# Second layer of a graph network: softmax chain moved three blocks behind the sums, four sum banks, and another order of stores

## What is computed

```python
h = jnp.maximum(_layernorm(x, axis=-1), 0.0)
m = jax.nn.relu(feat[src]) + EPS            # feat = h
ex = jnp.exp(logits - seg_max[dst])         # logits = m
denom = jax.ops.segment_sum(ex, dst, num_segments=N)
a = ex / denom[dst]
msg = jax.ops.segment_sum(a * m, dst, num_segments=N)
feats = feat + msg
x = x + (feats @ W + b)
```

## Time and profile before

| what | us |
|---|---|
| median of 3 runs | 2431.22 |
| lowest and highest of them | 2426.68, 2435.64 |
| the profiled execution | 2425.77 |
| its span | 2424.0 |
| POOL busy in the span | 1731.9 (71%) |
| DVE busy in the span | 1891.8 (78%) |
| PE busy in the span | 1792.9 (74%) |

### The profile page before, as it was taken

One profiled execution on the slowest core, in us unless ns is written; L12 is line 12 of the kernel. 1 busy time (PEld: TensorE's weight loads), 2 busy tenths in 40 slices (PEclk: granted clock), 3 DMA queues, 4 the chain that ended last, 5 costly groups with the idle time before them and its releaser, 6 DMA issues.

```text
span 2424.0 us, 54194 instructions
## 1 busy us (share of the span) xinstructions
PE 1792.9 (74%) x11221; PEld 1480.3 (61%) x11222; DVE 1891.8 (78%) x4571; ACT 762.8 (31%) x1322; POOL 1731.9 (71%) x1796
## 2 busy tenths in 40 slices
PE   3778777767676766777666767676776766899999
PEld 2466665656555555656555656565555654688887
DVE  8999998878787787887887878887888888454544
ACT  5001112222323333334444444444455556000000
POOL 4777777777777777777777777777777770477774
PEclk9899898988888888888888888888888887999999
DMA  5133444444434445454444445545554444877774
GB/s 165 42 94 91 110 102 104 123 105 113 126 102 124 122 108 137 111 140 127 123 136 128 132 130 139 139 130 137 137 137 136 138 127 142 314 264 270 264 273 149
DMA packets 172472, 344.69 MB, mean 142 GB/s; under 512 B 72689, under 2 KB 126763, under 8 KB 158078
## 3 DMA queue, kind: packets, MB, share of 16 engines
q1 hardware_dynamic: 33378, 153.14, 21.5%
q0 software_dynamic: 60864, 99.55, 17.4%
q10 hardware_dynamic: 77990, 89.82, 10.9%
HBM read 247.65 MB, written 94.68 MB: 141 GB/s over the span
## 4 chain that ended last, share of the span: by engine, by line
POOL 57%; issue 19%; PE 15%; DVE 2%; DMA 2%; ACT 1%; SPq 0%; POOLq 0%; DVEq 0%; ACTq 0%
POOL rows_buf L598 57%; PE ps L864 11%; PE ps L874 2%; DMA rows_buf<-table,index 1%; ACT features_buf L947 0%; PE ps L887 0%; PE ps L679 0%; PE ps L794 0%; DMA final<-residual 0%; DVE ps L1350 0%; PE ps L848 0%; SPq L535 0%; DVE zone L1387 0%; PE ps L881 0%; DMA table<-features_buf 0%
## 5 line engine op out<-in xcount | busy, mean ns | idle before, releaser
L598 POOL DMA_INDIRECT rows_buf<-table,index x1539 | 1493.7, 971 | 495.3 <-issue 492.6
L794 PE MATMUL ps<-zone,planes 128*128 128x400 f16 x2352 | 614.4, 377 | 538.4 <-DVE zone L1387 436.2
L1005 ACT ACTIVATE features_buf<-ps 128x800 f16<-128x800 f32 x392 | 327.8, 836 | 1216.0 <-PE ps L794 1211.1
L1387 DVE TENSOR_SCALAR zone<-iota_c,planes 128x400 f16<-128x400 int16 x2352 | 664.7, 336 | 57.6 <-issue 47.6
L794 PEld LDWEIGHTS ps<-zone,planes 128*128 128x128 f16 x2352 | 250.1, 106 | 715.3 <-issue 657.4
L679 PEld LDWEIGHTS ps<-wet,zone 128*128 128x128 f32 x3136 | 544.9, 248 | 43.6 <-issue 32.5
L679 PE MATMUL ps<-wet,zone 128*128 128x96 f32 x3136 | 531.9, 328 | 8.1 <-DMA zone<-edge_t 8.1
L666 PE MATMUL ps<-onehot,features_buf 128*96 128x128 f32 x3120 | 425.4, 282 | 0.0
L666 PEld LDWEIGHTS ps<-onehot,features_buf 128*96 128x96 f32 x3120 | 392.2, 173 | 11.1 <-issue 0.7
L1350 DVE TENSOR_TENSOR ps<-ps,rows_buf 128x768 f32<-128x768 f32 x171 | 164.6, 962 | 244.1 <-DMA rows_buf<-table,index 216.8
L1148 DVE TENSOR_TENSOR planes<-ps,planes 128x1536 f16<-128x1536 f32 x196 | 341.5, 1742 | 0.0
(11 more groups left out here) (187 smaller groups left out, 785.5 us busy)
## 6 DMA issues: line engine op xcount, KB each, us to landing
counts<-features_buf ACTq DMA_DIRECT2D x392, 200.0 KB
zone<-edge_t SPq DMA_DIRECT2D x98, 768.0 KB
single<-table SPq DMA_DIRECT2D x3072, 0.4 KB
rows_buf<-counts SPq DMA_DIRECT2D x24, 1600.0 KB
rows_buf<-table,index POOLq DMA_INDIRECT x1539
planes<-counts SPq DMA_DIRECT2D x12, 1600.0 KB
table<-planes SPq DMA_DIRECT2D x5, 840.0 KB
final<-residual ACTq DMA_DIRECT2D x48, 48.0 KB
```

The costliest lines, as they stand in the source:

```text
L598: nc.gpsimd.indirect_dma_start(out=into[:, t, :], out_offset=None, in_=table, in_offset=bass.IndirectOffsetOnAxis(ap=at[:, t:t + 1], axis= ...
L794: nc.tensor.matmul(count_ps[:, bass.ds(banks[k], WC)], row_hot[:, u % 2, g * GS + k, :], pair_hot[:, g * GS + k, :], start=False, stop=Fal ...
L1005: nc.scalar.activation(count_out[:, k], bank, ACT.Copy, accum_out=row_sum[:, bass.ds(p, 1)]).then_inc(moved, 1)
L1387: last = nc.vector.tensor_scalar(pair_hot[:, k, :], iota_c[:, :], step_pair[:, bass.ds(i * (IS * SC) + (u * SC + k), 1)], None, ALU.is_equal)
```

## The change

- PE makes `turn` three positions behind the sums instead of one, and `finish` four instead of two (`LAG = 3`). The sums go round four banks (0, 1, 6, 7) and wait for the softmax four positions back; the first four do not wait for any.
- DVE does `softmax(s)` and then `add_aggregate(s-3)` and `add_final(s-4)`. The softmax's result goes to a buffer of four slots, `update`.
- `own` moves from `zone` to `onehot_x`, which is free then, and `own` and `final` have eight slots (`BU`) instead of six.
- SP stores the table pieces first, then all own rows, then the residual. Its two loads of `own` are gone; ACT loads `own` for every position, and six positions ahead.

```diff
-BU = 6
-FEAT = 5760
+BU = 8
+LAG = 3
...
-        own = zone[:, FEAT:FEAT + BU * D].rearrange("p (u d) -> p u d", u=BU)
+        own = onehot_x[:, :, :].rearrange("p a b -> p (a b)")[:, 0:BU * D].rearrange("p (u d) -> p u d", u=BU)
+        block_bank = [0, 1, 6, 7]
...
                 sp.wait_ge(node_out, NG)
                 block_load(1)
+                for u in range(NU - 2):
+                    weighted_store(u)
+                block_load(2)
+                for u in range(NU - 2, NU):
+                    weighted_store(u)
+                for u in range(NU):
+                    own_store(u)
                 for part in (slice(0, EVEN), slice(EVEN, NP)):
                     sp.dma_start(residual.rearrange("(p j) d -> p j d", j=NJ)[part], xs[part, :, :]
                                  ).then_inc(residual_out, 16)
-                for u in range(NU - 2):
-                    own_store(u)
-                weighted_store(0)
-                weighted_store(1)
-                own_store(NU - 2)
-                weighted_store(2)
-                own_store(NU - 1)
-                block_load(2)
-                weighted_store(3)
-                sp.wait_ge(own_out, 2 * NU * 16)
-                sp.wait_ge(step_done, SC + NSTEP)
-                for b in range(2):
-                    sp.dma_start(own[:, b, :], own_rows[b * P:(b + 1) * P, :]).then_inc(residual_in[b], 16)
-                weighted_store(4)
                 for b in range(3, DB):
                     sp.wait_ge(block_ps, 2 + ORDER.index(b - 3) + 1)
                     block_load(b)
...
                     pe.wait_ge(block_in[b % 3], (b // 3 + 1) * 16)
-                    pe.wait_ge(soft_done, s + 1)
+                    if s > LAG:
+                        pe.wait_ge(soft_done, s - LAG + 2)
...
-                turn(0, 0)
-
                 for s in range(2, NB):
                     if ORDER[s] < DB:
                         block_sums(s, ORDER[s])
                     else:
                         fetched_sums(s, ORDER[s] - DB)
-                    turn(s - 1, s - 1)
-                    finish(s - 2, s - 2)
-                turn(NB - 1, NB - 1)
-                finish(NB - 2, NB - 2)
+                    if s >= LAG:
+                        turn(s - LAG, s - LAG)
+                    if s > LAG:
+                        finish(s - LAG - 1, s - LAG - 1)
+                for s in range(NB, NB + LAG):
+                    turn(s - LAG, s - LAG)
+                    finish(s - LAG - 1, s - LAG - 1)
                 finish(NB - 1, NB - 1)
...
-                    if s >= 2:
-                        act.dma_start(own[0:n, s % BU, :], own_rows[rows_at, :]).then_inc(residual_in[s % BU], 16)
+                    act.dma_start(own[0:n, s % BU, :], own_rows[rows_at, :]).then_inc(residual_in[s % BU], 16)
                     act.dma_start(final[0:n, s % BU, :], residual[rows_at, :]).then_inc(residual_in[s % BU], 16)
...
-                softmax(0, 0, 0)
-                softmax(1, 1, 0)
-                add_aggregate(0, 0)
-                for s in range(2, NB):
+                for s in range(NB):
...
                     softmax(s, s, 0)
-                    add_aggregate(s - 1, (s - 1) % 2)
-                    add_final(s - 2, s - 2, 0, min(P, N - ORDER[s - 2] * P))
-                add_aggregate(NB - 1, (NB - 1) % 2)
-                add_final(NB - 2, NB - 2, 0, min(P, N - ORDER[NB - 2] * P))
+                    if s >= LAG:
+                        add_aggregate(s - LAG, (s - LAG) % 2)
+                    if s > LAG:
+                        add_final(s - LAG - 1, s - LAG - 1, 0, min(P, N - ORDER[s - LAG - 1] * P))
+                for s in range(NB, NB + LAG):
+                    add_aggregate(s - LAG, (s - LAG) % 2)
+                    add_final(s - LAG - 1, s - LAG - 1, 0, min(P, N - ORDER[s - LAG - 1] * P))
                 add_final(NB - 1, NB - 1, 0, min(P, N - ORDER[NB - 1] * P))
```

More of the change, by code:

```diff
@@ L209, in gnn_kernel @@
         ln_eps = sb("ln_eps", [P, 2])
-        soft = sb("soft", [P, 2, 4, 2 * D])
+        soft = sb("soft", [P, 2, 3, 2 * D])
+        update = sb("update", [P, LAG + 1, D])
         rows = rows_buf[:, 0:RS * T * D].rearrange("p (s t d) -> p s t d", s=RS, t=T)
@@ L861, in block_sums @@
                     pe.wait_ge(block_in[b % 3], (b // 3 + 1) * 16)
-                    pe.wait_ge(soft_done, s + 1)
+                    if s > LAG:
+                        pe.wait_ge(soft_done, s - LAG + 2)
                     for j in range(NJ):
                         last = nc.tensor.matmul(
-                            ps[:, s % 2, 0:4 * D], blocks[b % 3][0:NP].rearrange("p (d j) -> p j d", j=NJ)[:, j, :],
+                            ps[:, block_bank[s % 4], 0:4 * D], blocks[b % 3][0:NP].rearrange("p (d j) -> p j d", j=NJ)[:, j, :],
                             table16[0:NP, j, :], start=(j == 0), stop=(j == NJ - 1))
@@ L871, in fetched_sums @@
                     pe.wait_ge(fetch_hot_done, g + 1)
-                    pe.wait_ge(soft_done, s + 1)
+                    if s > LAG:
+                        pe.wait_ge(soft_done, s - LAG + 2)
                     for k in range(FETCH[g]):
-                        last = nc.tensor.matmul(ps[:, s % 2, 0:4 * D], fetch_hot[g % 2][:, k, :],
+                        last = nc.tensor.matmul(ps[:, block_bank[s % 4], 0:4 * D], fetch_hot[g % 2][:, k, :],
                                                 fetched[g % 2][:, k, :], start=(k == 0), stop=(k == FETCH[g] - 1))
@@ L880, in turn @@
                     pe.wait_ge(soft_added, b + 1)
-                    nc.tensor.transpose(ps[0:D, 2 + u % 2, 0:P], soft[:, u % 2, 3, 0:D], ident[:, :]
+                    nc.tensor.transpose(ps[0:D, 2 + u % 2, 0:P], update[:, u % (LAG + 1), :], ident[:, :]
                                         ).then_inc(soft_turned, 1)
@@ L1547, in softmax @@
                     dve.wait_ge(block_ps, b + 3)
-                    found = ps[:, slot, 0:4 * D].rearrange("p (q h d) -> p q h d", q=2, h=2)
+                    found = ps[:, block_bank[u % 4], 0:4 * D].rearrange("p (q h d) -> p q h d", q=2, h=2)
                     nc.vector.tensor_copy(soft[:, slot, 1, :].rearrange("p (q d) -> p q d", q=2),
@@ L1564, in softmax @@
                     dve.wait_ge(soft_step[4], b + 1)
-                    nc.vector.scalar_tensor_tensor(soft[:, slot, 3, 0:D], total, 1.0 / P_SCALE,
+                    nc.vector.scalar_tensor_tensor(update[:, u % (LAG + 1), :], total, 1.0 / P_SCALE,
                                                    soft[:, slot, 2, D:2 * D], ALU.mult, ALU.mult
@@ L1569, in softmax @@
                     dve.wait_ge(residual_in[u % BU], (i + (u // BU + 1)) * 32)
-                    nc.vector.tensor_tensor(soft[:, slot, 3, 0:D], soft[:, slot, 3, 0:D], own[:, u % BU, :], ALU.add
+                    nc.vector.tensor_tensor(update[:, u % (LAG + 1), :], update[:, u % (LAG + 1), :], own[:, u % BU, :], ALU.add
                                             ).then_inc(soft_done, 1)
```

## The result

| | before | changed |
|---|---|---|
| median of 22 runs each, us | 2431.39 | 2437.87 |
| lowest and highest | 2425.28, 2437.36 | 2432.27, 2441.37 |
| span of the profiled execution | 2424.0 | 2434.2 |

The ratio is 1.0024, with a 95% interval of 1.0016 to 1.0032: 5.8 us slower, 3.9 to 7.8 (the two medians lie 6.5 us apart). The forecast was +4.3 us, 2435.5, within half a per cent.

The account below looks back on a forecast made before the run. PE was taken to set the pace in the second layer's steady part, so only the ends could change. The terms 3.3 + 0 + 1.0 gave +4.3 us, from 2431.22 to 2435.5 us, range 2425.6 to 2445.

Parts of the forecast that it names:

- The change does what it says: Rival, start of second layer: block 3 arrives in time, gain capped near 4 us, -3 with the end, 2428; chance 0.12.
- the idle time: Sign, PE before position 3: one idle time of 12 to 16 us, ended by block 3's DMA.
- the lower clock: Sign, position 3 after the stall: its first 3 us run at clock 0.50.
- The last sums near 2419.7: Sign, end of the second layer: the last sums near 2419.7 us, with four copies behind the last softmax.
- Term 1: Start of second layer: late block 3 moves position 4 from 2103.45 to 2106.75, +3.3 us (bounds -1.6 and +11.7).
- Term 2: Steady part of second layer: 0 us, since the four banks remove waits that were not there.
- Term 3: End, behind the last softmax: four copies and five additions instead of two and three, +1.0 us.
- Sharing: Rival, block 3's load: gathers and ACT's loads take turns with SP's queue; 2440.5 us, or 2443.9 at low rate; chance 0.20.
- late loads: Rival, softmax 0: twelve loads instead of eight compete with block 3, softmax done after 2106.7; 2437 us; chance 0.06.
- The cover for `turn(0)`: Start: softmax 0 done at 2100, ahead of the `turn(0)` of 2106.7 by over 6 us.
- lands some 3 us later: 40th gather, if block 3 came in time: issued at 2133.9, landing some 3 us later; PE would ask at 2128.4.
- the gain is capped near 4 us: Gathers limit any faster start: 3 us from the gathers' earlier start, about 1 of slack.

Follow-up runs that it names:

- e4: Changed kernel with the residual store put back into the gap ahead of the table pieces: 2428.02 us, 0.9991 of the kernel before.
- e3: Changed kernel with the load of count block 3 ahead of the own rows and the residual: 2443.35 us, 1.005 of the kernel before.
- e5: Changed kernel with 85 unused matmuls keeping PE busy while it waits for block 3: 2432.13 us, 1.0004 of the kernel before.
- e10: Changed kernel with turns and finishes caught up over the last positions, shortening the end: 3779.46 us on another chip, 0.9981 of the kernel before.
- e1: Changed kernel's lag of three and four banks, with the store order of before: 2434.46 us, 1.0021 of the kernel before.
- e6: e1 with every second gathered block one position later in the order: 2426.38 us, 0.9988 of the kernel before.
- e7: Changed kernel with own rows in the gap, residual last, and each engine waiting only for what it needs: 2426.68 us, 0.9991 of the kernel before.
- e8: e7 with the gathered-block order of e6: 2425.95 us, 0.9989 of the kernel before.
- e2: Changed kernel's store order with the chain of before (one block behind, two banks): 2446.42 us, 1.0068 of the kernel before.
- e9: e4 with the gathered-block order of e6 and a shorter end: 3778.78 us on another chip, 0.9978 of the kernel before.

## Why the prediction was right, and where its sizes were off

**The mechanism held step by step.** Position 2 ran at once at full clock. The stall moved behind it and became longer; SP's list put block 3 behind everything; the gap of the DMA engines stood empty. e4 moves one store into the gap and gets 8.7 us back at position 4, and e3 shows that exchanging block 3 with what stands ahead of it doesn't help. *The change does what it says* (0.12) fell with that. The number alone would not have told this mechanism from others: any cost of the start up to about +11 us stays within half a per cent. The rows tell it. Of the signs listed, the idle time was just longer than forecast (16.2 us, not 12 to 16) and the lower clock lasted nearly 6 us, not 3. "The last sums near 2419.7" fits only their end by the forecast's own +3.3 (2416.54 + 3.3); they ended at 2422.75 aligned.

**Term 1, forecast +3.3, measured +6.2.** Two parts:

- The start of position 3: 2097 forecast, 2098.4 aligned measured. The first table piece was issued at the same aligned time (2058.07 less 2.88 is 2055.19), so block 3 was there 41.5 us behind the first byte. The window of these 41.5 us, columns as in the earlier trace rows:

```profile
2059.80:2101.29 41.49, 25.26 (x146) 20.39 (x145) 12.96 (x29) 9.41 (x17) 10.18 (x11) 0.83 0.96 335
```

335 GB/s are 13.9 MB: the 12.88 of the forecast and 1.0 of others, where 0.8 had been estimated. So the sum as it was worked out, 2098.1 at 332 GB/s, was right within 0.3 us, and the miss is the step behind it, the choice of 2097 because the end might run at 366. By an estimate from the 358 GB/s that the Trainium skill's "DMA: Bandwidth & Descriptors", section "Specifications", gives as a core's limit to HBM, the 12.88 MB would have been there 5.5 us earlier than they came; the 335 GB/s of this window lie below that figure, and the 416 and 401 of two short windows below lie above it. +1.4.
- The cold clock. I took position 3's 9.73 us from the stall of before. It took 11.29. Windows of the changed kernel (PE busy, granted clock, DMA share, GB/s):

```profile
2101.00:2103.00 2.00, 1.71 (x6) 0.50 1.00 416
...
2105.00:2107.00 2.00, 2.00 (x8) 0.50 0.99 401
2107.00:2109.00 2.00, 2.00 (x12) 0.91 1.02 367
```

The 1.2 GHz level (0.50) lasts until about 2107, nearly 6 us, where it was 3 before. The cost above 8.29 is 3.0 us instead of 1.44, and e5 shows that it is the clock: 8.34 us warm. +1.5.

**Term 2, 0, held**: from position 4 to the last sums are 310.49 us in both traces, and the four banks removed nothing. **Term 3, +1.0, measured +1.1**; e10 takes it away.

**Sharing (0.20) did not happen, and late loads (0.06) came near.** The engines' time by queue in the changed kernel (packets, MB, share; q1 is SP's, q0 POOL's, q10 ACT's), first from 2088 to 2101, while block 3 moves, then from 2101 to 2107, when all three queues move packets throughout; the third fence is the kernel before, from 2082 to 2085:

```profile
q1 hardware_dynamic: 323, 4.10, 89.5%
q0 software_dynamic: 160, 0.35, 7.4%
q10 hardware_dynamic: 48, 0.02, 0.5%
```
```profile
q1 hardware_dynamic: 178, 2.05, 81.3%
q0 software_dynamic: 183, 0.38, 16.3%
q10 hardware_dynamic: 182, 0.06, 4.0%
```
```profile
q1 hardware_dynamic: 362, 1.07, 95.4%
q10 hardware_dynamic: 300, 0.10, 13.1%
```

SP's queue kept nine tenths, not a half. From 2101 to 2107 the three queues moved 178, 183 and 182 packets: as many each, but with SP's about 11.5 KB long, the gathers' 2.1 and ACT's 0.4, the shares were 81, 16 and 4%. The Trainium skill's rule that an engine takes turns packet by packet ("DMA: Bandwidth & Descriptors", "Queues, rings and completion order") agrees with these counts. But turns of unequal packets are no equal shares, which was my error in reading it. The loser is ACT, whose queue moves about 30 packets a microsecond there, where before, beside SP's packets of 3 KB, it moved 100. Softmax 0 needs the first two loads, 256 rows of 384 bytes. In DVE's timeline its wait for them ends here:

```profile
2109.89 0.26 DVE L1567 TENSOR_TENSOR update<-update,onehot_x 128x96 f32<-128x96 f32 x1 [32.36 <-DMA final<-residual]
```

That is 13.7 us after the issue of `final` at 2096.21, where it was 8.1 before (2084.59 less the 2076.46 of the earlier trace rows); in e5 it is 14.7. The cover for `turn(0)` at 2112.42 was 2.3 us, not "over 6". e5 uncovers it: with position 3 three microseconds shorter, `turn(0)` waits. The packet counts of the two traces show the starving; no run changed a packet size by itself.

**A wrong step that did not come to bear:** a gather's landing. I wrote that the 40th "lands some 3 us later". In e1 it took 6.9, with the same order of gathers. In the changed kernel PE reaches those sums only at 2149.83, so it didn't matter; but "the gain is capped near 4 us" was still too kind: e1, with a start 2.2 us ahead of before and gathers 1.5 us behind it (2089.07, aligned 2089.40, against 2087.89), ended 4.7 us slower. With gathers this near, a faster start of PE is given back.

Why e1's gather took 6.9 us where that of before took at most 3.9, no run tested, but the traces point to the same turns. In e1 SP issues a count block at 2138.13, together with that gather, and from 2138.8 to 2144.5 its 1.64 MB hold 80.2% of the engines' time while the gathers move 126 packets. Before, the block next to it had been issued at 2132.19, 4.6 us ahead of the gather, and from 2136.8 to 2140.7 the gathers moved 284 packets to SP's 48. Open is the difference between e5's trace and its time, and why the 50 sums behind a stall took 1.4 us more in one trace and 3.0 in another.

## What to carry to other kernels

A stall in which PE waits for a chain can be taken out by moving the chain back, but if the DMA engines are full in that stretch, the next transfer takes its place: count the bytes ahead of each following input from the first free microsecond, and ask first whether a reordering leaves the engines idle anywhere. One store of 2.3 MB, put back into a gap of 5 us, was worth 8 us here. Price the restart behind a stall as a range (1.4 to 3.0 us for these sums) and not by the one case at hand. Where several queues are full, count a small load by its packets and not by its bytes. And where two waits are a few microseconds apart, look at the second one before paying for the first.

## What was not expected of the hardware

- The cost of a restart at the lower clock level isn't ordered by the idle time before it. Over 8.29 us for the same 50 matmuls: 3.0 after 16.2 us idle (changed), 2.4 after 8.45 (e1), 1.7 after 8.74 (e4), 2.7 after 7.86 (e6), 1.7 after 3.83 (e7), 2.6 after 3.64 (e8), 0.05 after 0.53 (e3); and, with a `turn` ahead of the sums, 1.44 after 10.5 (before), 1.4 after 20.4 (e3) and 1.4 after 30.3 (e2).
- With three queues full the engines moved 178, 183 and 182 packets from them in 6 us, of 11.5, 2.1 and 0.4 KB. Shares of the time go by packet size: 81, 16 and 4%.
- A load of 48 KB in rows of 384 bytes was there for the softmax 13.7 to 14.7 us after its issue beside such packets, and 8.1 us beside packets of 3 KB.
- From issue to use a gather took at most 3.9 us in one run and 6.9 in another, at DMA shares of 0.81 and 0.89.
- The same program took 2430 us on two occasions and 3788 and 3874 us on two others. Each occasion was on another chip, but one of the 24 runs of the kernel before on the first of them took 4016 us too. In e9, from the bridge on, PE stands idle up to 2.5 us before single matmuls with no wait that the profile names, 135 us in all. The cause is open.
